# A gated attention and mixture-of-experts kernel: the shorter grouping of tokens, a product moved ahead of a peel and a peel moved behind the inversion

## The reference, cut

```python
xn = layernorm(x)                                   # x: 8 x 512 x 128
s = attention(xn)      # 8 heads of 16; out1 - lam * out2; layer norm; projection Wo
h = mod(xn[:, :2].sum(axis=1).astype(int32), 8)     # the routing of a token
sel = stack([h, mod(h + 1, 8)])
for e in range(8):
    w = any(sel == e, axis=1) / 2
    acc += w[:, None] * (relu(xn @ W1[e] + b1[e]) @ W2[e] + b2[e])
out = x + s * silu(acc)
```

## Time and profile before

| | us |
|---|---|
| median of 3 runs | 412.27 (411.48 to 412.47) |
| the profiled execution | 411.52 |
| its span | 409.6 |
| PE busy | 381.5 |
| DVE busy | 291.8 |
| ACT busy | 267.5 |
| POOL busy | 189.3 |

### The profile page before, as it was taken

How to read it: one execution, slowest core, us unless ns; L and a number is a source line. 1 busy time by engine, 2 the same in 40 slices (tenths; PEclk the granted TensorE clock), 3 DMA queues, 4 the chain that set the end, 5 groups by cost and what they waited for, 6 DMA issues and landing times.

```text
span 409.6 us, 8427 instructions
## 1 busy us (share of the span) xinstructions
PE 381.5 (93%) x2576; PEld 248.3 (61%) x2576; DVE 291.8 (71%) x758; ACT 267.5 (65%) x667; POOL 189.3 (46%) x262
## 2 busy tenths in 40 slices
PE   4996989999999999999999999999999999999993
PEld 2353876565775667766665668765676667764321
DVE  7787996656686757766676767866686767866884
ACT  3581756666765776576666767676766668675783
POOL 7944203454456543565355532663573444541200
PEclk9996999999999999999999999999999999999999
DMA  7975953263216451265105640346136141216740
GB/s 263 343 230 112 242 196 91 80 206 105 79 37 191 111 195 21 79 190 168 46 27 170 189 140 18 136 121 197 48 127 216 22 169 47 81 26 213 230 159 26
DMA packets 36945, 54.75 MB, mean 134 GB/s; under 512 B 6724, under 2 KB 25141, under 8 KB 36903
## 3 DMA queue, kind: packets, MB, share of 16 engines
q1 hardware_dynamic: 31456, 46.94, 34.6%
q0 software_dynamic: 3296, 6.76, 7.8%
q10 hardware_dynamic: 2151, 0.53, 0.6%
HBM read 15.59 MB, written 6.75 MB: 55 GB/s over the span
## 4 chain that ended last, share of the span: by engine, by line
PE 74%; DVE 7%; DMA 5%; ACT 4%; SPq 4%; issue 4%; POOL 1%; ACTq 0%; DVEq 0%; POOLq 0%
PE ring L1393 14%; PE pv_bank L1327 13%; PE ring L1414 12%; PE score L1289 12%; PE exp L1314 10%; PE ring L1251 3%; DVE neg_max L1049 3%; DMA xs<-xn_rows,inverse 3%; SPq L532 2%; PE ring L1335 2%; PE ring L1255 1%; PE ring L1353 1%; PE ring L1276 1%; PE ring L1375 1%; PE score L1264 1%
## 5 line engine op out<-in xcount | busy, mean ns | idle before, releaser
L1049 DVE TENSOR_REDUCE neg_max<-score 128x1 f32<-128x512 f32 x256 | 169.0, 683 | 72.3 <-PE score L1289 66.7
L1289 PE MATMUL score<-ks,qs 96*128 96x512 bf16 x256 | 98.3, 386 | 6.3 <-DVE neg_max L1049 6.0
L787 ACT ACTIVATE probs<-exp 128x512 f32<-128x512 f32 x124 | 72.5, 605 | 36.3 <-PE exp L1314 32.3
L787 ACT ACTIVATE xin<-exp 128x512 f32<-128x512 f32 x120 | 69.7, 604 | 38.5 <-PE exp L1314 38.1
L1314 PE MATMUL exp<-qs,ks 99*128 99x512 bf16 x244 | 91.7, 380 | 0.1
L825 ACT ACTIVATE hT<-ring,pair 128x128 f32<-128x128 f32 x256 | 73.4, 377 | 13.0 <-PE ring L1393 11.9
L1414 PEld LDWEIGHTS ring<-w_sb,hT 128*128 128x128 f32 x568 | 73.5, 191 | 10.4 <-issue 3.5
L1414 PE MATMUL ring<-w_sb,hT 128*128 (+1 forms) x568 | 75.4, 275 | 0.9 <-ACT hT L825 0.9
L1393 PEld LDWEIGHTS ring<-xsT,pair 128*128 128x128 f32 x512 | 66.3, 191 | 14.6 <-issue 8.1
L1393 PE MATMUL ring<-xsT,pair 128*128 128x128 f32 x512 | 68.2, 276 | 1.7 <-issue 1.2
L684 POOL TENSOR_SCALAR tanh<-tanh 128x128 f32<-128x128 f32 x32 | 17.2, 536 | 95.5 <-ACT tanh L845 95.2
(11 more groups left out here) (198 smaller groups left out, 417.4 us busy)
## 6 DMA issues: line engine op xcount, KB each, us to landing
pair<-table SPq DMA_DIRECT2D x32, 580.0 KB
qs<-parts SPq DMA_DIRECT2D x42, 128.0 KB
ks<-parts SPq DMA_DIRECT2D x42, 128.0 KB
xin<-_attn_hidden_states_dram SPq DMA_DIRECT2D x8, 256.0 KB, 4.4
table<-in_L_ffn_W_dram SPq DMA_DIRECT2D x2, 1024.0 KB, 9.2
w_sb<-in_L_ffn_W_dram SPq DMA_DIRECT2D x8, 256.0 KB, 10.4
xn_rows<-xn SPq DMA_DIRECT2D x8, 256.0 KB, 3.0
table<-_attn_hidden_states_dram SPq DMA_DIRECT2D x8, 256.0 KB, 5.4
```

Source lines behind the costliest of these rows:

```text
L787: a.activation(prob(n), exp_banks[n][:, :], ACT.Exp, scale=SCALE).then_inc(exp_done, 1)
L1049: v.tensor_reduce(neg_max[:, b % 2, col:col + 1], score_bank[n % 2][:, :], AX.X, ALU.max, negate=True).then_inc(max_taken, 1)
L1289: t.matmul(score_bank[n % 2][:, :], qs[0:MAX_ROW, b % STK, hh, c * P:(c + 1) * P], ks[0:MAX_ROW, b % STK, hh, :], start=True, stop=True).t ...
```

## The change

1. `LN_GROUPS`: (6, 8) becomes (6, 7) and (7, 8), six groups of powers. For the three groups whose batches GpSimd normalises, GpSimd no longer makes `shift` with the power; it makes it for all 16 columns at once, ahead of its first normalisation. The VectorE instruction that made the last group's `shift` is gone, and `v01` is now (x0 + x1 - 2 mean) * rstd.
2. `count_groups`: h stays whole numbers, so three casts go. `seen` is written one column further on than it is read (`work[:, 767]` is zero), so the subtraction of the one-hot behind the scan goes.
3. `find_tokens`: VectorE makes one plane of `token`, ScalarE the other (`in_tile` times the row), in the `tokens` step at -45.6; `invert` waits for both.
4. The `ones` step's three DMAs are issued by SyncE instead of ScalarE.
5. Times: the peel (0, 1, 2) moves behind the product of the counts (-55.25 to -48.65), the peel (1, 1, 2) behind the inversion (-45.2 to 5.1), batch 2's normalisation up on ScalarE (-49.9 to -56.3), the extra tiles' transposes up (TX 2.4 to 3), the extras and the third part of the groups up by a score, the tanh down by 0.3, a few others by less.

```diff
-LN_GROUPS = ((0, 1), (1, 2), (2, 4), (4, 6), (6, 8))
+LN_GROUPS = ((0, 1), (1, 2), (2, 4), (4, 6), (6, 7), (7, 8))
-NORM_AT = (-58, -56.4, -49.9, -47.93, -49.2, -49.1, -49, -48.95)
+NORM_AT = (-58, -56.4, -56.3, -47.93, -49.2, -49.1, -49, -48.95)
-PEEL_AT = (((-55.5, -55.3), (-55.4, -55.25)), ((-45.5, -45.3), (-45.4, -45.2)))
+PEEL_AT = (((-55.5, -55.3), (-55.4, -48.65)), ((-45.5, -45.3), (-45.4, 5.1)))
-TX, DX = 2.4, 3.2
+TX, DX = 3, 3.2
-TANH, GATE = 0.7, 1.84
+TANH, GATE = 1, 1.84
...
+                elif kind == "ones":
+                    sp.wait_ge(dve_consts, 1)
+                    for slot_b in range(STK):
+                        sp.dma_start(ks[MAX_ROW:KROWS, slot_b, :, :],
+                                     ones_bf[:, :].unsqueeze(1).to_broadcast([PARTS, HEADS, S])).then_inc(ones_stacked, 16)
...
-                    if end < B:
+                    if first not in POOL_NORM:
                         g.tensor_scalar(shift[:, tok], mv[:, tok, 0], -1.0, None, ALU.mult)
...
-                    pool.wait_ge(shift_ready, 1 + [b >= end for _, end in LN_GROUPS].index(False))
+                    if b == POOL_NORM[0]:
+                        tok = slice(C * b, NT)
+                        pool.wait_ge(rstd_ready, len(LN_GROUPS))
+                        link(g.tensor_scalar(shift[:, tok], mv[:, tok, 0], -1.0, None, ALU.mult))
+                        link(g.tensor_tensor(shift[:, tok], shift[:, tok], rstd[:, tok], ALU.mult))
...
+                elif kind == "tokens":
+                    act.wait_ge(in_tile_ready, 1)
+                    a.activation(token[:, 1, :, :, :], in_tile, ACT.Copy, scale=row_of[:, 0:1]).then_inc(token_ready, 1)
...
-                link(v.tensor_copy(n_abs[:, :], whole_i))
-                link(v.tensor_tensor(over, n_abs[:, :], v_abs[:, :], ALU.is_gt))
-                link(v.tensor_tensor(n_abs[:, :], n_abs[:, :], over, ALU.subtract))
-                link(v.scalar_tensor_tensor(h[:, :], sign[:, :], -1.0, n_abs[:, :], ALU.add, ALU.mult))
-                link(v.tensor_copy(whole_i, h[:, :]))
-                link(v.tensor_scalar(whole_i, whole_i, EXP - 1, None, ALU.bitwise_and))
-                link(v.tensor_copy(h[:, :], whole_i))
+                link(v.tensor_tensor(over, whole_i, v_abs[:, :], ALU.is_gt))
+                link(v.tensor_tensor(n_abs[:, :], whole_i, over, ALU.subtract))
+                link(v.scalar_tensor_tensor(h_i[:, :], sign[:, :], -1.0, n_abs[:, :], ALU.add, ALU.mult))
+                link(v.tensor_scalar(h_i[:, :], h_i[:, :], EXP - 1, None, ALU.bitwise_and))
...
-                v.tensor_tensor(seen[:, :, :], seen[:, :, :], onehot[:, :, :], ALU.subtract).then_inc(seen_ready, 1)
+                v.tensor_tensor_scan(work[:, 768:1024], work[:, 511:767], zeros,
+                                     0.0, ALU.add, ALU.add).then_inc(seen_ready, 1)
...
-                v.tensor_scalar(token[:, 1, :, :, :], in_tile, row_of[:, 0:1], None, ALU.mult).then_inc(token_ready, 1)
...
-                    pe.wait_ge(token_ready, 1)
+                    pe.wait_ge(token_ready, 2)
```

More of the change, by code:

```diff
@@ L60 @@
 INVERT_AT = -40
-EXTRAS_AT = 5.2
-GROUPS_AT = (9.05, 10.72, 13.05, 14.05)
+EXTRAS_AT = 4.7
+GROUPS_AT = (9.05, 10.72, 12.55, 14.05)
 STACKS_BEHIND = 1
@@ L727, in _ @@
                     act.dma_start(lnb_sb[:, :], ln_b.rearrange("(p a) -> p a", a=1)).then_inc(small_loaded, 16)
-                elif kind == "ones":
-                    act.wait_ge(dve_consts, 1)
-                    for slot_b in range(STK):
-                        act.dma_start(ks[MAX_ROW:KROWS, slot_b, :, :],
-                                     ones_bf[:, :].unsqueeze(1).to_broadcast([PARTS, HEADS, S])).then_inc(ones_stacked, 16)
                 elif kind == "copy_ninth":
@@ L860, in _ @@
             v.memset(zeros, 0.0)
+            v.memset(work[:, 767:768], 0.0)
             link(v.memset(va[:, :, :, :, HD:VW], 0.0))
@@ L945, in find_tokens @@
                 dve.wait_ge(slots_split, 1)
-                link(v.tensor_tensor(in_tile, by_pair(slot_tile[:, 0:NT], FT), over_pairs(columns[:, :, :], NT // 2), ALU.is_equal))
-                v.tensor_tensor(token[:, 0, :, :, :], in_tile, by_pair(ordinal[:, :], FT), ALU.mult)
-                v.tensor_scalar(token[:, 1, :, :, :], in_tile, row_of[:, 0:1], None, ALU.mult).then_inc(token_ready, 1)
+                v.tensor_tensor(in_tile, by_pair(slot_tile[:, 0:NT], FT), over_pairs(columns[:, :, :], NT // 2),
+                                ALU.is_equal).then_inc(in_tile_ready, 1)
+                dve.wait_ge(in_tile_ready, 1)
+                v.tensor_tensor(token[:, 0, :, :, :], in_tile, by_pair(ordinal[:, :], FT), ALU.mult).then_inc(token_ready, 1)
             def find_rows(q):
@@ L1014, in _ @@
                         continue
-                    tok = slice(C * first, C * end)
-                    v.tensor_tensor(v01[:, :], xin[:, :, 0], xin[:, :, 1], ALU.add).then_inc(pair_summed, 1)
-                    dve.wait_ge(rstd_ready, g + 1)
+                    link(v.tensor_tensor(v01[:, :], xin[:, :, 0], xin[:, :, 1], ALU.add))
                     dve.wait_ge(stats_ready, end)
-                    v.scalar_tensor_tensor(shift[:, tok], mv[:, tok, 0], -1.0, rstd[:, tok],
-                                           ALU.mult, ALU.mult).then_inc(shift_ready, 1)
+                    v.scalar_tensor_tensor(v01[:, :], mv[:, :, 0], -2.0, v01[:, :],
+                                           ALU.mult, ALU.add).then_inc(pair_summed, 1)
                 elif kind == "transpose_x" and s[1] not in PEELED:
```

27 lines of the change are left out of this document (12 added, 15 removed).

## The result

The changed kernel takes **415.15 us** (median of 4 runs, 414.93 to 415.55), the kernel before 412.37 (411.48 to 412.62): ratio 1.0079, 95% interval 1.006 to 1.0097. It is slower, by 2.8 us in the medians and by 3.3 in the ratio; the forecast was 1.4. The time lies just inside the forecast's range of 411.0 to 415.2. The profiled execution took 415.26 us with a span of 413.4 (before 411.52 and 409.6).

The account below looks back on a forecast made before the run. TensorE is busy for 93% of the span, so the head's chain to z of tile 0 was taken to set the end. +1.4 us, containing the 0.55 gained, on a median of 412.27 gave 413.7 us, range 411.0 to 415.2.

Parts of the forecast that it names:

- Powers: GpSimd's groups of powers: the split adds and the removed shifts save, so the last ends at 16.9 us as before; 0.
- The normalisations: GpSimd's sixteen normalisations, behind two operations over 16 columns: they end at 25.7 us instead of 25.1.
- VectorE's chain: VectorE's work from the powers to `at_row`: it ends at 27.95 us instead of 29.66, 1.7 us sooner.
- TensorE's head: TensorE's work up to the inversion's end, with ScalarE's 1248-column copy ahead: 30.05 us instead of 30.60, gain 0.55.
- The gather: The first tile's gather, waiting for `inverse` and eight stores: no cost from the stores, 0 to +1; landing at 35.8 us.
- sign of being wrong: First tile's landing before 35.3 or after 36.5 us, among the observations that would show the prediction wrong.
- The gather waits for a store: Rival: batch 3's store, behind the Pool stores and a stack part, lands 2 us late; +2.5 to +3.5, 415.3; chance 0.11.
- Behind the landing: TensorE from first tile's landing to score 8, peel at half clock: score 8 ends at 41.5 us against 40.07, +1.4.
- z: z of tile 0, the event said to set the end: done at 45.5 us, before at 44.13.
- The rest: Moved tanh and the extra tiles' transposes, against TensorE's later waits: 0, from -0.8 to +0.5 us.

Follow-up runs that it names:

- e3: The changed kernel, with VectorE waiting for GpSimd's last normalisation ahead of `in_tile`: 414.83 us, ratio 1.0067 to the kernel before.
- e10: The changed kernel with six later numbers set back, peel (1, 1, 2) in TensorE's wait for the gather, VectorE waiting for GpSimd's last normalisation: 409.61 us, ratio 0.9994.
- e9: The changed kernel with the six numbers that act behind the gather set back and peel (1, 1, 2) in TensorE's wait for the gather: 413.85 us, ratio 1.0082.
- e15: The changed kernel, with VectorE waiting for GpSimd's last normalisation, on one chip with three neighbours: 413.23 us, ratio 1.0030.
- e13: The changed kernel, with VectorE waiting for GpSimd's last normalisation and peel (1, 1, 2) at 4.5, in TensorE's wait for the gather: 412.34 us, ratio 1.0003.
- e6: The kernel before with only the change's numbers behind the gather (TX, EXTRAS_AT, GROUPS_AT, INIT_AHEAD, SPLIT_MAX, TANH): 412.96 us, ratio 1.0026.
- e16: The changed kernel, VectorE waiting for GpSimd's last normalisation, peel (1, 1, 2) in the gather wait, six later numbers set back, on another chip: 411.26 us, ratio 0.9992.
- e8: The changed kernel with peel (1, 1, 2) moved from 5.1 to 4.5, into TensorE's wait for the gather: 414.86 us, ratio 1.0069.
- e5: The changed kernel with batch 4 normalised by ScalarE and peel (1, 1, 2) at 2.5, in TensorE's wait for the gather: 412.26 us, ratio 1.0025.
- e14: The changed kernel itself, run again on one chip as base for three neighbours: 414.75 us, ratio 1.0070 to the kernel before.
- e12: The changed kernel, six later numbers set back, peel (1, 1, 2) in the gather wait, the ones' three transfers back on ScalarE's queue: 415.53 us, ratio 1.0118.
- e1: The kernel before with only peel (1, 1, 2) moved from -45.2 to 5.1, into TensorE's wait for the gather: 411.24 us, ratio 0.996.
- e17: The kernel before with peel (1, 1, 2) in the gather wait and ScalarE's ten small-weight loads moved to SyncE: 413.79 us, ratio 1.009.
- e4: The changed kernel with batch 4 normalised by ScalarE, leaving GpSimd twelve normalisations: 413.87 us, ratio 1.0048.
- e18: The kernel before with only peel (1, 1, 2) moved into TensorE's wait for the gather, repeated on another chip: 408.89 us, ratio 0.9984.

## Why the prediction was wrong, point by point

- **Powers, 0:** right; the last ends at 16.77 (16.88 before).
- **The normalisations "end at 25.7 instead of 25.1":** this is the step that failed. They end at 28.54. I added the two operations ahead of them and took the 8.19 us over from the earlier trace rows, though by the same text's own numbers `in_tile` now begins at 24.0, 1.7 us ahead of their end, and `at_row` follows it at once. And the trace of before has the two together on a smaller scale:

```profile
L640 POOL TENSOR_SCALAR xn<-xin,rstd,shift x16: 443/457/807, 16.9 to 24.6; 128x128 f32<-128x128 f32 x16
...
20.63 0.81 POOL L640 TENSOR_SCALAR xn<-xin,rstd,shift 128x128 f32<-128x128 f32 x1
...
20.43 0.75 DVE L909 TENSOR_TENSOR_SCAN hT<-hT 128x256 f32<-128x256 f32 x1
```

  (The first line gives the shortest, median and longest of the sixteen in ns.) Five of them took 0.61 to 0.81 us, each beside a two-input instruction of VectorE over 256 columns, and the other eleven 0.44 to 0.47. So contention of some 1.2 us was in the 8.19 already, and I read only their sum. A bound could be had from these rows: the three steps that moved onto the normalisations last 4.0 us on VectorE, so up to 4. It was 3.0. The Trainium skill says it, "SBUF — State Buffer", section "Who interferes with whom": a VectorE instruction with two SBUF inputs contends with a GpSimd instruction that reads SBUF, and the port pair that they share is an exclusive lock. The trace agrees: the normalisation from 25.12 on got through only behind three such instructions, the first of which it met running (2.56 us).
- **VectorE's chain, 1.7 sooner:** 1.44 (28.22 for 29.66), the casts and the subtraction gone as counted, 0.35 of it lost to the same contention (0.94, 0.94 and 2.51 us for 0.81, 0.81 and 2.42). That this gain would be worth nothing was half seen: TensorE and ScalarE end the inversion's wait. e3 gives VectorE 1.7 us back and moves the inversion by 0.06.
- **TensorE's head, gain 0.55:** 0.34 (it ends at 30.25, before 30.59). The copy of 1248 columns took 1.33 us (1.36 forecast), and TensorE waits 0.34 us for the part behind it, as written.
- **The gather, "no cost, 0 to +1", landing at 35.8:** the first transpose is at 38.02, behind the 36.5 that was named as a sign of being wrong. The rival "The gather waits for a store" named this store, its place behind the Pool stores and a stack part, 2 us late, and its price: +2.5 to +3.5, 415.3. That is what came, with a chance of 0.11; the only thing that spoke for it there was a margin of 0.2 us, and what makes a store late was not looked for. e10 against e9 shows the cause. The size of the landing is in part luck: the gather went out at 34.64 where the sum had 30.9, 3.7 us late (the store issued at 29.54 and not by 27.4, its transfer 3.85 us and not 3, and 1.2 us behind it), and rows that took 3.4 us and not 4.9 gave 1.5 of it back, which nothing in the prediction had counted.
- **Behind the landing:** from landing to the end of score 8 6.3 us (5.7 forecast, 6.8 as the end of the sum). The peel ran wholly at half clock, and the clock came back 5.8 us behind the landing instead of 4.35 (5.45 was the latest that the prediction gave if it came at all). Mechanism right, term 0.6 too small. In the whole change, with VectorE's wait, the peel's place costs 0.9 to 1.1 us (e15 against e13).
- **z, 45.5:** 48.40. 2.2 of the 2.9 us come from the landing, 0.6 from the term above.
- **The rest, 0 (-0.8 to +0.5):** e6 says +0.4 to +1.8; e16 against e13 has +0.5 to +1.1 in the middle, within the noise. So this term was too low. Which of the six numbers does it I have not tried. In the changed kernel's own trace the part from the first y rows on is 0.5 us shorter; so the cost lies ahead of them, if the traces can be set side by side here.

The forecast of +1.4 had the right sign, for half the reason: the peel and the clock are real, and the largest single part was a contention that it didn't count.

**What stays open.** Contention cost 3.6 to 4.2 us where the peel stands in the gap and the later numbers are off (e9, e10), 1.8 to 2.6 with batch 4's way (e8, e5), and 1.5 to 1.7 in the whole change (e14, e15). Why it is less there is open. That the late gather leaves a long thin stretch in which the clock is at half whatever stands there, so that the peel's place pays only when the gather is early, fits e8 and the clocks of the runs (with contention none lies above 0.992; without it and with the peel in the gap half or so lie at 0.994 or above, 5 to 9 of twelve). It is argued from these, not shown apart, and e8's slower rows would explain a part of e8 as well. The 1.20 us between the store's landing and the gather's issue stand in the profiles of e8, e9, e12 and e14 too (1.19 or 1.20), and in none in which `inverse` released it (0.29 in before, e1 and e3); what they are was not tried.

**A version that beats both:** e1, the peel alone in the gap, at 0.996 and 0.9984 of the kernel before in two groups; the second interval just reaches 1. e10 takes most of the change's edits and is no faster than before.

## What to carry to other kernels

When an edit speeds up one of VectorE and GpSimd, look at what it newly lies beside on the other, and count up to the whole length of VectorE's two-input instructions as lost to GpSimd (here 3.0 us of 4.4); the cheapest cure here was a wait on the engine that had slack. Look at the shortest and the longest of a group, not only at its sum: the contention stood in the trace of before. A matmul that is moved off a head's path should go into the hole ahead of the awaited transfer, not behind it (e1, e13). Small loads and broadcasts that are in flight with a gather delay it in these profiles, even from another queue, but moving them to where they are late for their own reader and stand in front of stores lost more (e17).

## What the runs showed of the hardware

- Sixteen 128x128 f32 normalisations on GpSimd: 7.95 us with VectorE's wide bf16 instructions held back (e3), 11.0 beside 4.4 us of them; one that takes 0.46 us took 2.56. Beside two-input f32 instructions over 256 columns one took 0.61 to 0.81 (before). VectorE's own became 4 to 16% longer.
- The runs of one kernel differ with the clock: e1 took 409.71 us with a mean granted clock of 1.0 and 414.71 with 0.985, e4 411.78 at 0.999 and 415.05 at 0.985. Whether and when the clock falls in the thin stretch at 33 to 44 us differs between executions (it fell at 32.2 in the profile of e14, 38.7 in e13's, not at all there in those of e4 and e18), and one profile shows one case.
- A gather's rows were in use 3.4 to 5.6 us after its issue. Those issued behind the last small load took 3.4 to 3.9 (the changed kernel, e14, e9), or 5.3 with the broadcasts of ones beside them (e12); with the small loads beside them it was 4.2 to 5.6, but for e4's 3.5; e17's, without them, took 3.7 at most.
